# The first norm of a token, attention, state and feed-forward tower folded into the weights behind it

## The reference

```python
x = emb[inp]                                        # 64 sequences of 128 tokens, 256 wide
q, k, v = x @ Wq.T + bq, x @ Wk.T + bk, x @ Wv.T + bv   # 16 heads of 16
ctx = softmax(q k^T / 4) v                          # no mask
h = ctx @ Wo.T + bo
n = layernorm(h)                                    # (h - mean) / sqrt(var + 1e-5)
a = scan_t( (n @ B_w.T) @ C_w.T , decay)            # exclusive scan along the sequence
h = h + sigmoid(n @ gate_w.T + gate_b) * a
h = h + layernorm(h) @ sign(weight).T
```

## Time and profile before

| | |
|---|---|
| median of 3 runs | 702.94 us (700.94 to 703.19) |
| the profiled execution | 703.16 us, of which the trace's span is 701.4 us |
| busy: PE, PEld | 647.6 us (92%), 611.2 us (87%) |
| busy: ACT, DVE, POOL | 606.9 us (87%), 577.8 us (82%), 407.8 us (58%) |
| granted clock of TensorE, mean | 0.969 of full speed |

### The profile page before, as it was taken

The page is one execution under the profiler, slowest core; times in us unless marked ns, Lnnn a source line. Parts: engine busy times, 40 slices in busy tenths (PEclk is TensorE's granted clock), DMA queues, the critical chain, the costliest instruction groups (busy, mean ns, idle before and its releaser), DMA issues. The chain is left out here.

```text
span 701.4 us, 21283 instructions
## 1 busy us (share of the span) xinstructions
PE 647.6 (92%) x6727; PEld 611.2 (87%) x6727; DVE 577.8 (82%) x1205; ACT 606.9 (87%) x2249; POOL 407.8 (58%) x463
## 2 busy tenths in 40 slices
PE   3578999999999999999999999999999999998863
PEld 2468899999999999999999999999999999998752
DVE  3456788888989898888998998888998998888742
ACT  2398999999999999999999999999999999999510
POOL 7410466765655666765655666776565565655552
PEclk9799999999999999999999999999999999999975
DMA  6323333223333333223333333233333333222000
GB/s 155 109 92 106 107 107 90 90 94 109 119 120 105 120 120 99 85 95 101 113 120 105 120 120 116 77 95 96 109 120 119 105 120 120 88 75 79 17 16 30
DMA packets 56161, 69.81 MB, mean 100 GB/s; under 512 B 6784, under 2 KB 41792, under 8 KB 56128
## 3 DMA queue, kind: packets, MB, share of 16 engines
q1 hardware_dynamic: 52048, 60.48, 25.1%
q0 software_dynamic: 3072, 8.39, 6.0%
q10 hardware_dynamic: 1008, 0.53, 0.4%
HBM read 10.65 MB, written 8.39 MB: 27 GB/s over the span
## 5 line engine op out<-in xcount | busy, mean ns | idle before, releaser
L392 ACT ACTIVATE probs<-ps_s,neg_max 128x128 f32<-128x128 f32 x1024 | 346.5, 409 | 36.5 <-DVE neg_max L527 36.4
L527 DVE TENSOR_REDUCE neg_max<-ps_s 128x4 f32<-128x512 f32 x256 | 175.9, 687 | 39.1 <-PE ps_s L676 30.2
L748 PE MATMUL ps_t<-ident,probs 128*128 128x128 f32 x1024 | 158.8, 278 | 11.8 <-ACT probsT L402 10.8
L402 ACT COPY probsT<-ps_t 128x512 f32<-128x512 f32 x256 | 165.9, 648 | 1.6 <-PE ps_t L748 1.6
L392 ACT ACTIVATION_READ_ACCUMULATOR probs<-ps_s,neg_max 128x1 f32 x640 | 146.7, 229 | 0.0
L748 PEld LDWEIGHTS ps_t<-ident,probs 128*128 128x128 f32 x1024 | 113.9, 141 | 36.7 <-issue 25.1
L676 PE MATMUL ps_s<-k_stack,q_stack 128*128 128x256 f32 x512 | 124.5, 324 | 6.1 <-DMA q_stack<-q_low 6.0
L318 POOL TENSOR_TENSOR state_high<-state_in,ones_col 128x512 fp32r<-128x512 f32 x32 | 33.3, 1040 | 163.5 <-DVE state_in L663 163.5
L304 POOL TENSOR_TENSOR xn<-h,mv 128x512 f32<-128x512 f32 x64 | 66.8, 1044 | 63.5 <-DVE ve L554 62.9
L560 DVE TENSOR_REDUCE row_sum<-probs 128x4 f32<-128x512 f32 x96 | 65.3, 680 | 28.3 <-ACT probs L392 28.3
L676 PEld LDWEIGHTS ps_s<-k_stack,q_stack 128*128 128x128 f32 x512 | 77.9, 192 | 7.2 <-DMA q_stack<-q_low 7.2
(11 more groups left out here) (120 smaller groups left out, 1886.9 us busy)
## 6 DMA issues: line engine op xcount, KB each, us to landing
k_stack<-k_high SPq DMA_DIRECT2D x128, 128.0 KB, 2.5
q_stack<-q_high SPq DMA_DIRECT2D x64, 256.0 KB, 2.4
k_stack<-k_low SPq DMA_DIRECT2D x64, 128.0 KB, 2.3
q_stack<-q_low SPq DMA_DIRECT2D x32, 256.0 KB, 2.5
out<-y SPq DMA_DIRECT2D x32, 256.0 KB, 2.1
x_emb<-in_emb,id_col POOLq DMA_INDIRECT x64, 3.7
raw<-in_wkT SPq DMA_DIRECT2D x1, 256.0 KB, 3.2
raw<-in_wqT SPq DMA_DIRECT2D x1, 256.0 KB, 4.2
```

The costliest lines, as they stand in the source:

```text
L392: last = nc.scalar.activation(probs[s % 2][:, j], ps_s[s % 2][:, j * SEQ:j * SEQ + SEQ], ACT.Exp, bias=neg_max[s % 2][:, j:j + 1], accum_o ...
L402: nc.scalar.copy(probsT[st][vp if st < AHEAD else 0][:], ps_t[:]).then_inc(act_pT, 1)
L527: nc.vector.tensor_reduce(neg_max[s % 2][:], ps_s[s % 2][:].rearrange("p (h k) -> p h k", h=HPS), axis=AX.X, op=ALU.max, negate=True).then ...
L748: last = nc.tensor.transpose(ps_t[:, j * SEQ:j * SEQ + SEQ], probs[st % 2][:, j], ident[:])
```

## The change

Mean and deviation of the first norm are taken out of the tokens. With the contexts c, h0 = c Wo^T + bo and the norm (h0 - mean) r, with r the inverse deviation of a token. Subtracting the mean is linear, so it is done once on Wo and bo (rows minus their mean), and the centred Wo is multiplied once with the gate's weights and with the product of the state's two. Gate and state are then products of `ctxT` and the folded weights; behind them `gate_row` or `state_row` (the folded bo) is added and the result is scaled by r: POOL makes `gate_bias` = `gate_row` r + gate bias in two operations, DVE makes `gate_in` from it in two instructions of 256 columns, and `state_in` from `state_mid` (the product plus `state_row`) in two more, each with r as a scalar for each partition. `xn1`, its four transposes, `xn1Th` and `xn1Tl` are gone.

The folding stands in `prepare` of PE, ACT and DVE ahead of turn 0; twelve of its matmuls have plain fp32 operands. ACT writes the high parts of the folded weights, DVE the low parts, and turn 0's product of v waits for them.

The order of a turn is laid out anew. PE: `ffn` ahead of T(0) and into `g1`; state's product in step 1, from `ctxT`; `k` into `g3`; gate's product in step 5; transposes of `xn2` in step 6 (before step 7); the sum over time in step 6 of the same turn instead of step 1 of the next. ACT: the copy of step 5 ahead of `q_high`, `ctxTh` behind the exponentials of step 5, `xn2Th` ahead of those of step 6, and the wait of `ctxTh` is extended to the gate's and state's products. SP loads Wo first of the second three weights.

```diff
-                if exists(t - 2):
-                    await_event(pool, dve_ve1, 1, t - 2, 1)
-                    normalise(t - 2, t - 3, h0[par], mv1, ve1, rs1, xn1, pe_xn1T, centred1, rs1_done, pool_xn1)
...
+                if exists(t - 2):
+                    await_event(pool, dve_ve1, 1, t - 2, 1)
+                    await_event(pool, dve_in, 1, t - 3, 1)
+                    await_event(pool, dve_gate, 1, t - 3, 1)
+                    scale(t - 2, ve1, rs1, rs1_done)
...
+                if exists(t - 2):
+                    await_event(pool, rs1_done, 1, t - 2, 1)
+                    nc.gpsimd.tensor_tensor(gate_bias[:], gate_row[:].unsqueeze(1).to_broadcast([P, 2, D]),
+                                            rs1[:].unsqueeze(2).to_broadcast([P, 2, D]), ALU.mult).then_inc(bias_step, 1)
+                    await_event(pool, bias_step, 1, t - 2, 1)
+                    nc.gpsimd.tensor_tensor(gate_bias[:], gate_bias[:], gb_row[:].unsqueeze(1).to_broadcast([P, 2, D]),
+                                            ALU.add).then_inc(pool_bias, 1)
...
+                if exists(t - 2):
+                    await_event(pool, dve_in, 1, t - 2, 1)
+                    await_event(pool, pe_sums, 1, t - 3, 1)
+                    nc.gpsimd.tensor_tensor(state_high[:], state_in[:], ones_col[:].unsqueeze(2).to_broadcast([P, 2, D]),
+                                            ALU.mult).then_inc(state_highs, 1)
+                    await_event(pool, state_highs, 1, t - 2, 1)
+                    nc.gpsimd.tensor_tensor(state_low[:], state_in[:], state_high[:].bitcast(fp32),
+                                            ALU.subtract).then_inc(state_lows, 1)
+                gather(t + 2, par)
...
                 move_probsT(4)
-                move_block(t - 2, xn1T[0], g3, pe_xn1T, pe_state, act_xn1T)
                 move_inverse(t - 1)
...
                                              bias=bq_col[:, c:c + 1]).then_inc(act_qhi, 1)
-                move_probsT(5)
+                exponentials(5)
                 move_ctx(t - 1)
-                exponentials(5)
                 move_probsT(6)
...
+            nc.vector.tensor_reduce(row_mean[:, 0:C], raw[0][:], axis=AX.X, op=ALU.add).then_inc(means_made, 1)
+            dve.wait_ge(small_loaded, 112)
+            nc.vector.tensor_reduce(row_mean[:, C:C + 1], bo_row[:], axis=AX.X, op=ALU.add).then_inc(means_made, 1)
+            dve.wait_ge(means_made, 2)
+            for c in range(C):
+                nc.vector.scalar_tensor_tensor(wo_cent[:, c], row_mean[:, c:c + 1].to_broadcast([P, D]), -1.0 / D,
+                                               raw[0][:, c], ALU.mult, ALU.add).then_inc(wo_centred, 1)
...
-                dve.wait_ge(small_loaded, 112)
+                dve.wait_ge(fold_made, 1)
+                nc.vector.tensor_copy(gate_row[:], g3[:, 0:D]).then_inc(rows_copied, 1)
+                nc.vector.tensor_copy(state_row[:], g3[:, D:2 * D]).then_inc(rows_copied, 1)
+                low_part(wg, ps_c[:].rearrange("p (c o) -> p c o", c=C), 5)
...
+                if exists(t - 2):
+                    await_event(dve, pe_state, 1, t - 2, 1)
+                    nc.vector.tensor_tensor(state_mid[:], g0[:].rearrange("p (b d) -> p b d", b=2),
+                                            state_row[:].unsqueeze(1).to_broadcast([P, 2, D]), ALU.add).then_inc(dve_mid, 1)
+                if exists(t - 2):
+                    await_event(dve, dve_mid, 1, t - 2, 1)
+                    await_event(dve, rs1_done, 1, t - 2, 1)
+                    await_event(dve, state_lows, 1, t - 3, 1)
+                    for b in range(2):
+                        last = nc.vector.scalar_tensor_tensor(state_in[:, b], state_mid[:, b], rs1[:, b:b + 1], powers_tok[:],
+                                                              ALU.mult, ALU.mult)
+                    last.then_inc(dve_in, 1)
+                maxima(4)
                 sums(3)
...
+                if exists(t - 2):
+                    await_event(dve, pe_gate, 1, t - 2, 1)
+                    await_event(dve, pool_bias, 1, t - 2, 1)
+                    await_event(dve, act_tanh, 1, t - 3, 1)
+                    for b in range(2):
+                        last = nc.vector.scalar_tensor_tensor(gate_in[:, b], g1[:, b * D:b * D + D], rs1[:, b:b + 1],
+                                                              gate_bias[:, b], ALU.mult, ALU.add)
+                    last.then_inc(dve_gate, 1)
+                low_features(t - 3, xn2T, g3, act_xn2T, pe_ffn, dve_xn2lo)
...
+            def prepare():
+                pe.wait_ge(wo_centred, 3)
+                pe.wait_ge(ws_copied, 1)
+                for k in range(C):
+                    for c in range(C):
+                        at = (2 * k + c) * P
+                        nc.tensor.transpose(ps_c[:, at:at + P], wo_cent[:, c, k * P:k * P + P], ident[:])
+                    last = nc.tensor.transpose(ps_t[:, D + k * P:D + k * P + P], bo_cent[:, k * P:k * P + P], ident[:])
...
+                pe.wait_ge(raw_loaded[1], 32)
+                pe.wait_ge(dve_xlo, 1)
+                for dst, row, src in ((ps_c, 0, raw[1]), (g2, D, ws_raw)):
+                    for c in range(C):
+                        for k in range(C):
+                            mm(dst[:, c * D:c * D + D], wo_turned[:, k, c * P:c * P + P], src[:, k], k == 0, k == C - 1)
+                    for k in range(C):
+                        last = mm(g3[:, row:row + D], bo_turned[:, k, 0:P], src[:, k], k == 0, k == C - 1)
+                last.then_inc(fold_made, 1)
...
                 if exists(t - 4):
                     await_event(pe, dve_xn2lo, 1, t - 4, 1)
-                    await_first((dve_in, 1, t - 3, 1), (dve_gated, 1, t - 4, 1))
-                    token_major(g0, [wf_sign], xn2T, [(0, 0), (0, 1)], pe_ffn)
+                    await_first((dve_gate, 1, t - 3, 1), (dve_y, 1, t - 5, 1))
+                    token_major(g1, [wf_sign], xn2T, [(0, 0), (0, 1)], pe_ffn)
+                attention(0)
                 if exists(t):
+                    if isinstance(t, int) and t == 0:
+                        pe.wait_ge(w_low, 6)
                     await_first((dve_h0, 1, t - 2, 1), (dve_v, 1, t - 1, 1))
                     token_major(g2, wv, xT, PARTS, pe_v)
...
+                if exists(t - 2):
+                    await_first((dve_gated, 1, t - 3, 1), (dve_qlo, C, t, C))
+                    token_major(g0, ws, ctxT, PARTS, pe_state)
...
                 attention(3)
                 if exists(t + 1):
                     await_event(pe, dve_xlo, 1, t + 1, 1)
-                    await_first((dve_gate, 1, t - 3, 1), (dve_klo, C, t, C))
-                    feature_major(g1, wk, xT, pe_k)
-                if exists(t - 2):
-                    await_event(pe, pool_xn1, 1, t - 2, 1)
-                    await_first((dve_xlo, 1, t + 1, 1), (dve_xn2lo, 1, t - 4, 1))
-                    to_features(g3, lambda b: xn1[:, b], pe_xn1T)
+                    feature_major(g3, wk, xT, pe_k)
...
                 if exists(t + 1):
-                    await_first((dve_gated, 1, t - 3, 1), (dve_in, 1, t - 3, 1), (dve_qlo, C, t, C))
+                    await_event(pe, dve_xlo, 1, t + 1, 1)
+                    await_first((dve_mid, 1, t - 2, 1), (dve_qlo, C, t, C))
                     feature_major(g0, wq, xT, pe_q)
...
                 if exists(t - 2):
-                    await_event(pe, dve_xn1lo, 1, t - 2, 1)
-                    await_first((dve_klo, C, t + 1, C), (dve_gate, 1, t - 3, 1))
-                    token_major(g1, wg, xn1T, PARTS, pe_gate)
+                    await_first((dve_y, 1, t - 4, 1), (dve_gate, 1, t - 3, 1))
+                    token_major(g1, wg, ctxT, PARTS, pe_gate)
                 attention(6)
-                if exists(t - 2):
-                    await_first((dve_qlo, C, t + 1, C), (dve_gated, 1, t - 3, 1))
-                    token_major(g0, ws, xn1T, PARTS, pe_state)
-                attention(7)
                 if exists(t - 3):
                     await_event(pe, pool_xn2, 1, t - 3, 1)
+                    await_first((dve_klo, C, t + 1, C), (dve_xn2lo, 1, t - 4, 1))
                     to_features(g3, lambda b: xn2[:, b], pe_xn2T)
+                if exists(t - 2):
+                    await_event(pe, state_lows, 1, t - 2, 1)
+                    await_first((dve_qlo, C, t + 1, C), (dve_mid, 1, t - 2, 1))
+                    mm(g0[:], earlier[:], state_high[:].rearrange("p b d -> p (b d)"), True, False)
+                    mm(g0[:], earlier[:], state_low[:].rearrange("p b d -> p (b d)"), False, True).then_inc(pe_sums, 1)
+                attention(7)
                 if exists(t - 1):
                     await_event(pe, dve_ctxlo, 1, t - 1, 1)
                     token_major(g2, wo, ctxT, PARTS, pe_o)
```

(49 more changed lines are left out.)

114 lines of the change are left out of this document (40 added, 74 removed).

## The result

The changed kernel takes **735.12 us** (733.08 to 737.88) against 702.38 us of the kernel before in the same comparison: a ratio of 1.047, 95% interval 1.043 to 1.051. It is slower by 33 us; 698 was forecast, and the range ended at 711.

A forecast was written before the change was run, and what follows sets the result against it. It took ACT's chain from S(3) to T(7), closed by PE's work to the next S(3), to bound each turn. Loop -7.2, start +4, end -2 sum to -5.2 against 703.16, giving 698 us; range 685 to 711.

The forecast's parts named there:

- SP's stack DMAs start with `k_high` as before: In each turn, SP's stack DMAs were to start with `k_high` unchanged; no time was added for them.
- DVE blocked by POOL: Rival: in each turn `state_in` on DVE waits for POOL's second-norm operations; 712 us, chance 0.22.
- The ring: One loop turn: S(3) to T(7) 8.52 us plus T(7) to the next S(3) 10.89, together 19.41.
- The loop's gain: Turns 2 to 31: thirty turns, each 0.24 us shorter, -7.2 us.
- The cover of 0.23 on DVE: Before exponentials 5: DVE's maxima allow them at S(3) + 5.89, ACT is due at S(3) + 6.12, 0.23 us spare.
- Ahead of turn 0: Start: twelve fp32 folding matmuls, then DVE's row copies and low parts, delay the first maxima; +4 us, +1 to +7.
- the price of 0.85: Start: each fp32 folding matmul of 256 columns takes some 0.85 us at the lower clock level, twelve take 10.2.
- The end: From the last pair's `h0` on: norm work leaves, some 4 us; Wo's later product costs some 2; -2 us, -5 to +1.
- PE's own work is the limit: Rival: in the loop the copy of step 6 is no wait, since ACT starts exponentials 3 earlier; 690 us, chance 0.22.
- 18.8 for PE's own work: Loop turn if ACT were no limit: 19.57 us less 0.35 for four transposes and about 0.4 of waits, 18.8.

The follow-up runs named there:

- e1: The changed kernel with a turn's two gathers and their id copies moved to the head of POOL's turn, held until step 0's scores are done: 723.44 us.
- e3: The changed kernel with `ve` made by two DVE instructions of one column each instead of one of two columns: 720.39 us.
- e4: The changed kernel with the edits of e1 and e3 together: 701.40 us, ratio 0.998 to the kernel before.
- e7_copy_ahead: e4 with ACT's copy of step 6 ahead of `ctxTh`, Wo's high-part products before the low-part ones, and `gate_in` ahead of `ctxTl`: 695.55 us.
- e8: e4 with Wo's product of the last pair ahead of the transposes of `xn2` and the sum over time: 698.01 us.

## Why the prediction was wrong

- **The step that failed, first**: "SP's stack DMAs start with `k_high` as before". They do, but of the moved steps the prediction costed the operations of POOL and not the gathers. They went from ahead of the stack DMAs to among them, and `q_low` lands late for S(0). The prediction gave this nothing; it costs 11.7 us by e1, and 19 by e3 against e4.
- **The step that failed, second**: DVE's `ve` was taken as unchanged. Before, none of POOL's arithmetic ran beside it, at most the issue of a gather, and all 64 took 0.169 to 0.173: POOL's `xn` waited for it. Now `h` and `gate_bias` run there. The prediction gave this nothing either; it costs 14.7 us by e3, and 22 by e1 against e4. The rival "DVE blocked by POOL" had the mechanism and the wrong place: in the loop `state_in` stands between POOL's operations of 512 columns, beside `rs` of two columns (309.26 to 309.96), and isn't held by it (the pair at 309.40 took 0.88, the pair of `gate_in` 0.87). The rival's 712 had neither the wait of `ve` nor the late landing in it. Near the end `state_in` itself is blocked: in e4_both a pair took 2.56, beside `gate_bias` at 675.71 and `xn` at 676.93.
- **The ring was right**: 8.52, 10.89, 19.41 forecast; 8.53, 10.83, 19.36 in e4_both. In the changed kernel the second was 10.86 without the wait for `q_low`. The loop's gain was 6.1 us (623.3 to 617.2) for a forecast of 7.2. The cover of 0.23 on DVE, where the prediction saw its greatest risk, held: in e4_both exponentials 5 start at S(3) + 6.21, right behind `q_high`, with no wait for the maxima.
- **Ahead of turn 0**: +4 forecast (from +1 to +7), +3.8 measured (30.0 to 33.8). S(0) was to stand at 31.9 and did at 31.11. The range was real: the twelve matmuls took 6.7 us in the changed kernel, the first four of them at the lower clock (granted 0.50, 0.85 us each), and 5.0 in e7_copy_ahead at the full one (0.42 each). The row that the price of 0.85 was taken from doesn't give it: two matmuls took 2.07 there, in a stretch where the profile has the granted clock at 1.00. The price came out all the same.
- **The end**: -2 forecast, +1.1 measured (+0.8 in e4_both). By e4_both both parts were mis-sized: from `h0` of the last pair to the end it is 30.3 instead of 33.3, 3.0 less and not 4; and `h0` comes 3.8 later and not 2 (18.6 behind the last maxima, 14.8 before). By e8, 3.5 of this is Wo's place behind the sum over time. About 1.0 of it is the clock: PE was busy 0.61 and 1.12 us of the stretches 660 to 663 and 663 to 666, and then ran most of that product at a granted clock of 0.50 (666 to 669), at a pitch of 0.21, where the kernel before ran it at 1.00, at 0.12.
- With the three terms as measured in e4_both, -6.1 + 3.9 + 0.8 = -1.4 against the profiled execution before: without the two failed steps the change is worth next to nothing (e4_both 0.998), since its start and end spend most of what the loop gains. Of the 3.8 us that this is off the forecast of -5.2, 2.8 are the end and 1.1 the loop. The rival "PE's own work is the limit" was wrong: ACT's copy was a wait, and once ACT's chain was shorter by 0.4 (e7) PE still waited 0.44 a turn for DVE. Its 18.8 for PE's own work was right.

## What to carry to other kernels

Moving an operation in an engine's order moves everything behind it on that engine, its DMAs and its meetings with another engine too: list for each queue what it issues beside what, before and after, and ask of each DMA whose landing has little slack. A wait of a tiny instruction on a shared resource costs as much as a large one's; look for it by comparing the duration of every form between two profiles, not only the busy shares. And where two losses hide each other, remove both before judging either: alone they gave back 12 and 15 us, together 34.
